# Two cross-attention and feed-forward layers: attention of all batches first, then the feed-forward part, instead of a loop over groups of eight batches

## The reference

```python
x = x + xattn0(layernorm(x), ctx)   # 16 heads; keys = values = rope(ctx), latent width 64
x = x + moe0(layernorm(x))          # 16 experts of width 128 and a shared one, top 4 within 2 of 4 groups
x = x + xattn1(layernorm(x), ctx)
x = x + ffn1(layernorm(x))          # width 704, top 2 of 8 low-rank adapters of rank 16
```

## Time and profile before

| | us |
|---|---|
| median of 3 executions | 3398.19 (3393.26 to 3401.04) |
| profiled execution, its own time | 3397.9 |
| its span, first to last instruction | 3396.1 |

### The profile page before, as it was taken

How to read it: one execution, slowest core, us unless ns; L and a number is a source line. 1 busy time by engine, 2 the same in 40 slices (tenths; PEclk the granted TensorE clock), 3 DMA queues, 4 the chain that set the end, 5 groups by cost and what they waited for, 6 DMA issues and landing times. The chain is left out here.

```text
span 3396.1 us, 43529 instructions
## 1 busy us (share of the span) xinstructions
PE 2958.6 (87%) x16008; PEld 1691.4 (50%) x16008; DVE 2015.0 (59%) x2351; ACT 1262.0 (37%) x1747; POOL 1759.2 (52%) x1008
## 2 busy tenths in 40 slices
PE   7689978899888998879998699878998799779988
PEld 6444456444465444754446444354445344454435
DVE  3576556766567674676655566455655565455645
ACT  3134434244341443423443334323442244323432
POOL 0467724677336774366763167504761277216750
PEclk9789989899988999898998799998998799888999
DMA  7423213233123331142321423104311332132310
GB/s 256 120 62 91 59 41 95 74 82 82 35 80 88 75 84 47 61 112 58 84 56 50 111 60 78 57 10 98 79 35 49 87 74 57 52 74 60 79 57 6
DMA packets 117806, 247.54 MB, mean 73 GB/s; under 512 B 30415, under 2 KB 82879, under 8 KB 110038
## 3 DMA queue, kind: packets, MB, share of 16 engines
q1 hardware_dynamic: 117590, 244.57, 27.1%
HBM read 171.24 MB, written 48.27 MB: 65 GB/s over the span
## 5 line engine op out<-in xcount | busy, mean ns | idle before, releaser
L1218 POOL TENSOR_TENSOR sums<-sums,prob 125x896 f32<-125x896 f32 x528 | 1117.9, 2117 | 141.8 <-ACT prob L1105 88.5
L1334 DVE TENSOR_REDUCE maxpart<-pair 112x2 f32<-112x1000 f32 x720 | 861.5, 1197 | 444.2 <-PE pair L854 444.1
L1105 ACT ACTIVATE prob<-wide 125x896 f32<-125x896 f32 x768 | 704.6, 917 | 882.8 <-PE wide L880 882.8
L895 PE MATMUL single<-prob,kv 125*64 125x448 f32 x3072 | 756.0, 571 | 0.9
L875 PE MATMUL wide<-qhigh,kparts 64*125 64x448 f32 x3072 | 461.9, 379 | 0.0
L854 PE MATMUL pair<-kparts,qhigh 64*112 64x500 f32 x1440 | 356.9, 491 | 61.7 <-DVE maxpart L1334 48.4
L854 PEld LDWEIGHTS pair<-kparts,qhigh 64*112 64x112 f32 x1440 | 129.1, 175 | 489.2 <-DVE maxpart L1334 398.4
L1218 POOL TENSOR_TENSOR sums<-prob 125x896 f32<-125x896 f32 x64 | 134.9, 2108 | 411.7 <-ACT prob L1105 411.7
L875 PEld LDWEIGHTS wide<-qhigh,kparts 64*125 64x125 f32 x3072 | 283.4, 187 | 110.0 <-issue 81.2
L880 PE MATMUL wide<-shift,ones_row 64*125 64x448 f32 x1536 | 289.8, 372 | 46.4 <-DMA shift<-maxrow 46.4
L875 PE MATMUL wide<-qlow,kparts 64*125 64x448 f32 x1536 | 288.2, 370 | 0.0
(11 more groups left out here) (322 smaller groups left out, 4235.4 us busy)
## 6 DMA issues: line engine op xcount, KB each, us to landing
kparts<-keys_merged SPq DMA_DIRECT2D x64, 750.0 KB, 9.1
wexp_low_values<-in_experts SPq DMA_DIRECT2D x68, 384.0 KB, 3.1
kparts<-kparts SPq DMA_DIRECT2D x96, 250.0 KB, 3.1
keys_merged<-kparts SPq DMA_DIRECT2D x32, 750.0 KB, 7.6
recip<-zrec_merged SPq DMA_DIRECT2D x112, 112.0 KB, 2.8
raw<-in_ctx SPq DMA_DIRECT2D x33, 375.0 KB
w_low_values<-w_merged SPq DMA_DIRECT2D x64, 192.0 KB, 3.3
values_merged<-kv SPq DMA_DIRECT2D x32, 375.0 KB
```

What stands on the lines that cost most here:

```text
L895: mm = pe.matmul(mix_acc[64 * half:64 * half + DC, 0:HQ], kv[:, j % 3, t, :], prob[:, (j * LT + t) % NPROB, half * HQ:(half + 1) * HQ], st ...
L1105: nc.scalar.activation(prob[:, n_ % NPROB, :].rearrange("p (a b) -> p a b", a=2), acc[0:LP, :, 0:HQ], ACT.Exp)\
L1218: nc.gpsimd.tensor_tensor(dst, first_in, prob[:, n_ % NPROB, :], ALU.add).then_inc(s["pool_sum"], 1)
L1334: V.tensor_reduce(maxpart[:, j % 2, t:NMAX:4, b], acc[0:TQ, :, 0:LB], AX.X, ALU.max).then_inc(*R.signal_drained(kind, *key))
```

## The change

- The program is unrolled. The parts are four blocks with a barrier after each: attention of layer 0, experts, attention of layer 1, feed-forward part of layer 1. Each goes through all four groups g. The tokens stay in SBUF (`x_all`, loaded during setup); `x_mid` and the block ahead of each loop are gone.
- Attention: the last `mix`, `context`, `norm`, `spread` and `share` of a group are placed among the queries of the next, and its `attn` in four pieces between the `smax` steps that end them. The layer norm of group g + 1 and its first `wsplit` steps are placed in the score tiles of the group's last batch; its first head weights are loaded one batch before.
- Layer 0: `rotate` two tiles sooner (t = 9, was 11), `ropecos` two (t = 10 and 11, was 0 and 1), `rope` one (t = 1 and 2), `keyT` two (t = 3 to 5, was 5 to 7), and over the borders of the groups, so that from the second group on the keys of a group's first two batches are made in the group before. The load of the next raw context follows `keyT`, as before. In a group's last batch GpSimd sums up to tile 6 (`POOL_LAST` 7, was 5).
- Experts: all 17 experts' weights stay in SBUF, loaded and split once. The norm and the nine parts of the ranking for group g + 1 are placed one after each expert of group g. The first group's come ahead of its first experts.
- Layer 1's feed-forward part: weights loaded and split once, at the start of the block (before: loaded from the end of each pass's attention on). Norm, routing, `mask`, `lora` and `tokw` of group g + 1 are placed in the six blocks of group g.
- The `table_probe` activations, which brought in ScalarE's function table for exp or sqrt ahead of its use, are gone.

The core of the diff (the step lists; the engines' parts of each step stay as they were, with counts over all groups in the waits, and with two buffers where a group's data meets the next one's):

```diff
-POOL_TILES, POOL_LAST = 11, 5
+POOL_TILES, POOL_LAST = 11, 7
...
-            if layer == 0 and t == LT - 1 and j + 3 < BG:
-                add("rotate", j + 3)
-            if layer == 1 and t == 2 and 2 < j + 2 < BG:
-                add("fetch", j + 2)
...
-            if layer == 0 and t in (5, 6, 7) and j + 2 < BG:
-                keys(j + 2, t - 5)
...
-            if layer == 0 and t in (0, 1) and j + 2 < BG:
-                add("ropecos", j + 2, t)
-            if layer == 0 and t in (2, 3) and j + 2 < BG:
-                add("rope", j + 2, t - 2)
...
+    for g in range(G):
+        first, old = BG * g, BG * g - 1
+        if layer == 0:
+            for n in range(H + 1):
+                if n + SPLIT_AHEAD < H:
+                    add("wsplit", g, n + SPLIT_AHEAD)
+                if n < H:
+                    add("qwide", g, n, region=n % 2)
+                if g and n == 0:
+                    add("mix", old, LT - 1)
+                    add("context", old)
+                if g and n == 1:
+                    add("norm", old, region=3)
+                if n < H:
+                    add("qrope", g, n)
+                if n >= 3 and n % 2:
+                    add("query", g, (n - 3) // 2, region=2)
...
+                if g and n == 5:
+                    add("spread", old)
+                if g and n == 8:
+                    add("share", old, 2)
...
+            for i in range(3):
+                maximum(first + 1, i, (0, 1, PAIR)[i])
+            add("query", g, NPAIR - 1, region=2)
+            if g:
+                add("attn", g - 1, 0, region=1)
+            for c in range(3):
+                add("smax", first, 3, c, region=(0, PAIR, 0)[c])
+            if g:
+                add("attn", g - 1, 1)
+                add("attn", g - 1, 2)
+            add("maxneg", first)
+            maximum(first + 1, 3)
+            add("maxT", first, region=3)
+            if g:
+                add("attn", g - 1, 3)
+        else:
+            for p in range(NPAIR):
+                if p + SPLIT_AHEAD < NPAIR:
+                    add("wsplit", g, p + SPLIT_AHEAD)
+                add("query", g, p, region=p % 2)
+                if g and p == 0:
+                    add("mix", old, LT - 1)
+                    add("context", old)
...
+                    add("norm", old, region=3)
+                if g and p == 6:
+                    add("spread", old)
...
+            for n in range(4, 9):
+                add("smax", first, n // 3, n % 3, region=(PAIR, 0, 0)[n % 3])
+                if g and n == 4:
+                    add("share", old, 2)
+                if g and n == 6:
+                    add("attn", g - 1, 0, region=1)
+            if g:
+                add("attn", g - 1, 1)
+            for c in range(3):
+                add("smax", first, 3, c, region=(PAIR, 0, 0)[c])
+            if g:
+                add("attn", g - 1, 2)
+            add("maxneg", first)
+            for i in range(2):
+                maximum(first + 1, i, (PAIR, 0)[i])
+            add("maxT", first, region=3)
+            if g:
+                add("attn", g - 1, 3)
+            for i in range(2, 4):
+                maximum(first + 1, i, (PAIR, 0)[i % 2])
...
+            for t in range(LT):
+                ahead = (j + 1, t + EARLY_MAX) if t + EARLY_MAX < LT else (j + 2, t + EARLY_MAX - LT)
...
+                if layer == 0 and t == LT - 3 and b + 3 < NB:
+                    add("rotate", b + 3)
...
+                if layer == 0 and t in (3, 4, 5) and b + 2 < NB:
+                    add("keyT", b + 2, t - 3, region=3)
...
+                if layer == 0 and t >= LT - 2 and b + 3 < NB:
+                    add("ropecos", b + 3, t - LT + 2)
+                if layer == 0 and t in (1, 2) and b + 2 < NB:
+                    add("rope", b + 2, t - 1)
+                if g + 1 < G and j == BG - 2 and t == 4:
+                    add("heads", g + 1)
+                if g + 1 < G and j == BG - 1:
+                    if t == 2:
+                        add("mean", g + 1, region=3)
+                    if t in (3, 4):
+                        add("square", g + 1, t - 3)
+                    if t == 5:
+                        add("var", g + 1, region=3)
+                    if t in (7, 8):
+                        add("rstd", g + 1, t - 7)
+                    if t == 9:
+                        add("xsplit", g + 1)
+                    if t == 10:
+                        for n in range(SPLIT_AHEAD):
+                            add("wsplit", g + 1, n)
...
+    for u in range(G * (E0 + 1)):
+        g, i = divmod(u, E0 + 1)
+        if g == 0 and i + SPLIT_AHEAD <= E0:
+            add("esplit", i + SPLIT_AHEAD)
+        add("gateup", u, region=u % 2)
+        if i == 0:
+            if g:
+                add("rank", g, RANKS - 1)
+            else:
+                for n in range(RANKS):
+                    add("rank", g, n)
+        if i == 1:
+            add("cwT", g)
+        if i:
+            add("weight", u, region=3 + i % 2)
+        add("hidden", u)
+        if u:
+            add("down", u - 1)
+        if u and i == 0:
+            add("out", g - 1)
+        if g + 1 < G and i and i - 1 < 7 + RANKS:
+            ahead(g + 1, i - 1)
+    add("down", G * (E0 + 1) - 1)
+    add("out", G - 1)
...
+        add("gateup", u, 0, region=0)
+        if more and m == 0:
+            add("mean", g + 1)
+        if more and m == 1:
+            add("var", g + 1)
+        if more and m == 2:
+            add("route", g + 1)
+        if more and m == 4:
+            add("mask", g + 1)
+        if more and m == 5:
+            add("lora", g + 1)
+        if u:
+            add("down", u - 1)
+        add("gateup", u, 1, region=1)
+        if u and m == 0:
+            add("loradown", g - 1)
+            add("out", g - 1)
+        if more and m == 0:
+            for n in (1, 2):
+                norm_schedule(add, g + 1, n)
+        if more and m == 1:
+            for n in (4, 5, 6):
...
+        if more and m == 3:
+            add("rank", g + 1, 2)
+            add("rank", g + 1, 3)
...
+    wexp_low = buf("wexp_low", [128, NE, 3 * D], F32R)
+    wexp_high = buf("wexp_high", [128, NE, 3 * D], F32R)
...
+            for i in range(NE):
+                sp.dma_start(wexp_in[:, i, :], a["experts"][i]).then_inc(s[f"expert_loaded_{i}"], 16)
...
-    nc.all_engine_barrier(sems_to_clear=setup_range)
-
-    with nc.Fori(0, G) as g:
```

More of the change, by code:

```diff
@@ L42 @@
 EPS = 1e-5
-WSLOT = 4
+NB = G * BG
+RANKS = 9
 EARLY_MAX = 4
@@ L65, in schedule, with maximum @@
     steps = []
+    heads = (H, NPAIR)[layer]
     def add(kind, *key, region=None):
         steps.append((kind, key, region))
[L69 to L80, removed]
+    def maximum(b, n, region=PAIR):
+        add("smax", b, n % 4, n // 4, region=region)
@@ L170, in schedule @@
-    add("mix", *last)
-    add("context", BG - 1)
-    add("norm", BG - 1, region=3)
-    for part in (0, 2, 1, 3):
-        add("share", BG - 1, part)
-    add("attn", region=0)
-    if layer == 0:
-        for i in range(2):
-            add("esplit", i)
-    add("mean", 0, region=2)
-    add("var", 0, region=5)
+        for part in range(2):
+            add("rope", 0, part)
     for part in range(2):
@@ new lines, in attention_schedule, with norm_schedule @@
+    add("mix", NB - 1, LT - 1)
+    add("context", NB - 1)
+    add("norm", NB - 1, region=3)
+    for part in (0, 2, 1, 3):
+        add("share", NB - 1, part)
+    for piece in range(4):
+        add("attn", G - 1, piece, region=None if piece else 1)
+    return steps
+def norm_schedule(add, g, step):
+    if step == 0:
+        add("mean", g)
+    elif step in (1, 2):
+        add("square", g, step - 1)
+    elif step == 3:
+        add("var", g)
+    elif step in (4, 5):
+        add("rstd", g, step - 4)
+    else:
+        add("xsplit", g)
@@ new lines, in ffn_schedule, with add @@
+def ffn_schedule():
+    steps = []
+    places = {"mean": 1, "var": 1, "route": 1, "mask": 1, "lora": 1, "tokw": 0}
+    def add(kind, *key, region=None):
+        steps.append((kind, key, places.get(kind, region)))
+    for n in range(7):
+        norm_schedule(add, 0, n)
+    add("wsplit")
+    add("route", 0)
+    for n in range(4):
+        add("rank", 0, n)
+    add("mask", 0)
+    add("lora", 0)
+    add("tokw", 0)
+    for u in range(G * MT):
+        g, m = divmod(u, MT)
+        more = g + 1 < G
+        add("gateup", u, 0, region=0)
[20 more added lines that the diff above has]
+            for n in (4, 5, 6):
+                norm_schedule(add, g + 1, n)
+        if more and m == 2:
+            add("rank", g + 1, 0)
+            add("rank", g + 1, 1)
+        if more and m == 3:
+            add("rank", g + 1, 2)
+            add("rank", g + 1, 3)
+        if more and m == 5:
+            add("tokw", g + 1)
+    add("down", G * MT - 1)
+    add("loradown", G - 1)
+    add("out", G - 1)
```

2307 lines of the change are left out of this document (1253 added, 1054 removed).

## The result

The changed kernel takes 3258.46 us (median of 4 executions, 3247.3 to 3259.59) against 3399.61 for the kernel before; the ratio is 0.9576, interval 0.9547 to 0.9606. The forecast was 3121, its range 3065 to 3200. So the direction was right, the size was not: 138 us are missing, and the time lies outside the range. The profiled execution has a span of 3256.6 us against the 3119 of my sum.

The account below looks back on a forecast made before the run. PE was taken to bound tiles, experts and blocks, latency the seams. Block by block, running totals 1411.5, 1760 and 2807 us plus 312.5 gave a span of 3119, time 3121 us; range 3065 to 3200.

Parts of the forecast that it names:

- The seams: Stretches between a pass's parts, bound by latency: in layer 0, 10.2 us restart and 31 us between scores and experts.
- four bare starts: Block starts left uncovered by PE's work after unrolling: 17, 17, 17 and 30 us.
- Rival 5: Whole kernel slower than before, because PE falls to the 1.2 GHz level under load; 277 us lost; chance 2%.
- Rival 4: ScalarE pays a 1.38 us drain at each of 36 function table switches, unhidden: 3171 us; chance 4%.
- (d): Layer 0 attention scores: sooner `keyT` lets `spread`'s store find the queue empty; `shift` waits fall 7 us a group, 1.4 left.
- Hidden work on VectorE: Moved VectorE (DVE) work mostly fits beside PE; experts' norm and ranking bounded from nothing to 9 + 14 us a group.
- rival 1: Hidden norm, ranking or `attn` pieces delay PE through in-order engine queues: +75 us, 3195 us; chance 20%.
- three times 10: Layer 1's feed-forward block: new PE waits around `loradown`, `tokw`, `lora` and `route`, 10 us for each of three groups.
- ±0: Layer 1's query stretches, groups 1 and 2: `attn`, `norm` and `mix` fill 8.5 us idle and a 4.2 us wait, adding nothing.
- The two starts: Layer 0's attention: heads at 127 us, with 6 for tables; last block: first feed-forward block at 30 us.
- +175: High ends together of the bounds on hidden norm and ranking, `attn` in query stretches, and feed-forward waits.

Follow-up runs that it names:

- e2: Kernel before the change, with only the sooner tiles of `rotate`, `ropecos`, `rope` and `keyT` in layer 0, within each group: 3420.37 us, ratio 1.006.
- e4: Changed kernel with `ropecos` in layer 0 at tiles 6 and 7 instead of 10 and 11: 3213.45 us, ratio 0.9452.
- e1: Changed kernel with layer 0's `rotate`, `ropecos`, `rope` and `keyT` back at their old tiles: 3260.89 us, ratio 0.958.
- e7: Changed kernel with `ropecos` at 6 and 7, `keyT` at 4 to 6, plus unused matmuls in the last block's gaps: 3219.14 us, ratio 0.9471.
- e8: Changed kernel with `ropecos` at 6 and 7, `keyT` at 4 to 6, and the last block's steps placed anew: 3193.53 us, ratio 0.9389.
- e12: e4 with e8's last block, plus layer 1's `spread`, `share` and first `attn` pieces sooner in the query stretch: 3163.42 us, ratio 0.9296.
- e3: Changed kernel with `keyT` in layer 0 one tile later (4 to 6): 3222.67 us, ratio 0.9479.

## Why the prediction was wrong, step by step

**What held.** The seams went beside PE's work and four bare starts are left. Layer 0's tail came out at 21.3 for 21.5, layer 1's first group at 250.1 for 249.6, its start at 16.2 for 16.7, the experts at 342 for 348.5. The wait for `cwT` is 14.2 us, once (10 to 20 forecast). Rival 5 is out for the changed kernel: the clock is 0.95 in each layer's first attention group and 0.97 to 0.98 in the other six. Rival 4 is out too. ScalarE's timeline in the first expert group:

```profile
1489.63 1.28 ACT L1334 ACT_TABLE_LOAD   x1
1490.92 0.22 ACT L1334 ACTIVATE moe_rt<-pair 112x64 f32<-112x64 f32 x1
```

The drain of 1.38 us that rival 4 goes by does not show between load and next activation, as in the earlier trace rows. 23 of the profile's 47 loads stand 0.02 us behind one activation and 0.01 us ahead of the next.

**The step that failed first: (d), "−7 a group" for `shift`.** Its mechanism was right, the waits fell from 32.9 to 5.0 us. What was wrong was to book the end of a wait as a gain: the same edit alone made the kernel before 20 us slower (e2). It brought `share` and `ropecos` together ahead of the reduction that PE needs next, and `share` into GpSimd's additions, where its median was 2.23 us. The question that the text of the prediction should have answered is who is late next. The gain was there to be had: e4, with the same sooner tiles but `ropecos` at 6 and 7, has 5.7 us of waits for `shift` where e1 has 40.9, and is 47 us faster than e1. In the same window as the earlier trace rows, before, `share` waited for its reciprocals seven times, 18.4 us in all (second row), and its median is the 0.63 us of an undisturbed operation:

```profile
L1395 DVE TENSOR_TENSOR ctx_n<-ctx_raw,recip x7: 625/626/756, 1156.5 to 1326.3; 128x448 f32<-128x448 f32 x7
its engine sat idle before it (us, times) until:
  DMA recip<-zrec_merged: 18.4, 7
```

There the reciprocals were 2.6 us late, and so was `shift`, while GpSimd ran out of `prob` tiles behind the waiting PE. In the changed kernel both come sooner, and `share` falls into GpSimd's run of additions.

**Hidden work on VectorE.** I counted VectorE's free time per tile and took each operation at its undisturbed length. Here such an operation, with two SBUF inputs, lasts until GpSimd's running instruction is over and 0.48 us more. I had the sign of it in the earlier trace rows, a comparison of 2.72 us where another takes 1.23, and used it for the ranking alone. It is rival 1 in kind, its cause not being the moved work but the port. Moving two operations of 0.55 us gives back 45 of layer 0's 57 us (e4), and its groups 1 and 2 then have score windows of 237 us, where the forecast had 238; their query stretches are still 2 to 3 us over the 82 forecast. The 0.7 us for `keyT` behind `rope`, about 19 us in all, I had not seen: `rope` now stood one tile ahead of it and no longer two.

**The last block: "three times 10" of waits.** The idle time was about right: 4.2, 3.9, 2.3 and 1.7 + 1.1 us a group, 13 for 10. Not in the sum was the clock behind each of them. I had written of the seams that work there runs at 1.2 GHz behind idle stretches, and then left it out for the waits that I added myself. e7 gives it 21 us of the 44, e8 shows that with most waits gone too 48 come back.

**Layer 1's query stretch, "±0".** It is 47.4 us, where the one before is 32.3. I had `attn` fill 8.5 us of idle time. It didn't: PE is busy for 35.7 us and still idle for 11.7. VectorE's timeline in that stretch suggests the reason:

```profile
2111.87 1.20 DVE L1120 TENSOR_REDUCE maxpart<-wide 112x2 f32<-112x1000 f32 x1 [3.28 <-PE wide L853]
2113.64 1.20 DVE L1120 TENSOR_REDUCE maxpart<-wide 112x2 f32<-112x1000 f32 x1 [0.57 <-PE wide L853]
2117.26 1.20 DVE L1120 TENSOR_REDUCE maxpart<-pair 112x2 f32<-112x1000 f32 x1 [2.41 <-PE pair L853]
```

A piece of `attn` holds PE for 3 to 5 us, and VectorE has nothing to reduce meanwhile. Then PE waits for reductions again. Pieces of that size don't fill waits of 0.6 us. Two of the four pieces, behind waits of over 2 us, also took 4.9 us in place of 3.3. Putting them sooner gave 1.5 us a group (e12); smaller pieces weren't tried, so this cause is argued and not shown. The stretch is 15 us over the forecast, the score tiles behind it are 6 us under (216.2 for 222.3, the wait of 4.2 us for `shift` ahead of them is gone). In sum the three groups with such a stretch are 9, 8 and 7 us over, which is all of the error in layer 1's attention.

**The two starts.** In layer 0 the tables land 13 us after their issue, and the squares of the norm stand behind `ropecos` in VectorE's queue (PE waits 13.4 us for them). I had 6 for the tables. In the last block PE waits 12.4 us for the ranking, and its timelines (VectorE, then GpSimd) show the port again:

```profile
2905.40 3.18 DVE L1817 TENSOR_SCALAR ffn_mask<-ffn_rt 112x32 f32<-112x32 f32 x1
2908.61 3.08 DVE L1818 TENSOR_TENSOR ffn_tokm<-ffn_mask,ffn_score 112x32 f32<-112x32 f32 x1
```

```profile
2905.37 3.16 POOL L1744 TENSOR_TENSOR ffn_w_up<-ffn_w_up_values,ffn_w_up_high 128x1408 fp32r<-128x1408 f32 x1
2908.50 3.14 POOL L1744 TENSOR_TENSOR ffn_w_gate<-ffn_w_gate_values,ffn_w_gate_high 128x1408 fp32r<-128x1408 f32 x1
```

Two operations of 32 columns take 3.1 us each, as long as the weight splits beside them; another pair of the same form took 0.18 and 0.62 just before. Holding the splits back until the ranking is done wasn't tried.

**The range.** Its high end of 3200 came from rival 1 with half of the upper bounds (3195). The bounds in full (+175) would have held the result, but by luck: the largest miss, `share` and `ropecos` in layer 0's scores, is in none of them, for both were put at nothing.

## What to carry to other kernels

A wait that ends last hides the ones that end just before it. Before a gain is booked for taking it away, look up at the same spot when every other input of the waiting instruction is ready. Where VectorE is near a deadline and GpSimd runs long operations, place VectorE's two-input SBUF work by GpSimd's phase, or cut GpSimd's instructions in halves: the length to plan with is its own plus that of GpSimd's instruction. And add to each idle stretch of PE the work that follows at the low clock.

## What the hardware showed that was not expected

- A VectorE instruction with two SBUF inputs that meets a running GpSimd instruction ends 0.48 us (`share`, 448 columns) or 0.42 us (`ropecos`, 384) behind it, whatever it lasts: 0.63 us alone, up to 2.58 in this kernel. The PSUM reductions (1.20 us) show nothing of it. The one-input TENSOR_SCALAR of 32 columns above does (3.18 us).
- A placement edit acts through phase. With VectorE's work unchanged, four places of two steps gave 3258, 3223, 3213 and 3238 us.
- In groups 1 to 3 of the last block, each idle stretch of PE of 1.7 to 4.2 us was followed by 5 us at 0.50 to 0.69 of the full clock; in group 0 one of 2.4 us was not. Behind the 19 border waits of up to 1.6 us in e3 none followed; behind the 19 of 1.5 to 2.0 us in the changed kernel 8 did.
- 56 unused matmuls a group made the kernel 19 us faster.
